# Sums of squares in a gated linear attention: one folded tile and a moved half of a product, in place of two sets of products

## The reference

```python
q, k, v, z = _silu(x @ Wq), _silu(x @ Wk), _silu(x @ Wv), x @ Wz
q, k, v = (causal depthwise convolution over 4 tokens of each)
q = q * cos + rot_half(q) * sin                      # rotary positions, k likewise
q = q / jnp.maximum(jnp.linalg.norm(q, axis=-1, keepdims=True), 1e-12)
k = k / jnp.maximum(jnp.linalg.norm(k, axis=-1, keepdims=True), 1e-12)
for s in range(4):                                   # a token looks at itself and 3 before it
    attn = einsum('bshd,bshd->bsh', q, lag(k, s)) * D ** -0.5
    out = out + (attn * sigmoid(lag(a, s) * b))[..., None] * lag(v, s)
out = out * rsqrt(mean(out * out) + eps) * norm_w * _silu(z)
return out @ Wout
```

## Time and profile before

| | us |
|---|---|
| median of 3 runs | 1094.22 |
| lowest and highest | 1091.1, 1095.05 |
| profiled execution, its own time | 1098.17 |
| its span (first to last instruction) | 1096.4 |
| busy PE, DVE, ACT, POOL in the span | 1013.1, 751.6, 557.3, 285.8 |
| mean granted PE clock | 0.956 |

### The profile page before, as it was taken

How to read it: one execution, slowest core, us unless ns; L and a number is a source line. 1 busy time by engine, 2 the same in 40 slices (tenths; PEclk the granted TensorE clock), 3 DMA queues, 4 the chain that set the end, 5 groups by cost and what they waited for, 6 DMA issues and landing times.

```text
span 1096.4 us, 16891 instructions
## 1 busy us (share of the span) xinstructions
PE 1013.1 (92%) x5736; PEld 804.0 (73%) x5736; DVE 751.6 (69%) x1305; ACT 557.3 (51%) x1105; POOL 285.8 (26%) x246
## 2 busy tenths in 40 slices
PE   6989999999999999999979999999997996679985
PEld 4778988998898854354469989889885454368875
DVE  4778999899899768972377877877874154524333
ACT  2558877877887787711155555655542023022321
POOL 1034234424423401030112122121100005536660
PEclk9989999999999999989989999999998998789996
DMA  7087867877877940430011011110002002178955
GB/s 223 3 218 152 190 154 154 175 163 158 168 162 171 248 106 0 155 86 0 1 58 58 29 57 29 57 57 29 29 0 73 0 1 87 70 222 272 278 159 183
DMA packets 81565, 121.59 MB, mean 111 GB/s; under 512 B 25123, under 2 KB 58734, under 8 KB 80880
## 3 DMA queue, kind: packets, MB, share of 16 engines
q1 hardware_dynamic: 69488, 86.91, 26.5%
q0 software_dynamic: 12032, 34.11, 15.7%
HBM read 70.31 MB, written 38.08 MB: 99 GB/s over the span
## 4 chain that ended last, share of the span: by engine, by line
PE 78%; DVE 10%; DMA 4%; ACT 3%; issue 3%; POOL 2%; SPq 0%; ACTq 0%; POOLq 0%; DVEq 0%
PE psum L647 9%; PE psum L649 9%; PE psum L648 9%; PE psum L872 5%; PE psum L1055 5%; PE psum L701 5%; PE psum L1014 5%; PE psum L819 4%; PE psum L897 3%; PE psum L779 3%; PE psum L760 3%; PE psum L1065 2%; PE psum L828 2%; PE psum L690 2%; DVE arena L1513 2%
## 5 line engine op out<-in xcount | busy, mean ns | idle before, releaser
L1513 DVE SCALAR_TENSOR_TENSOR arena<-arena,par_in 128x1024 f32<-128x1024 f32 x144 | 183.5, 1283 | 33.1 <-ACT arena L1138 23.5
L647 PE MATMUL psum<-G_r,arena_r 128*128 128x512 f32 x320 | 132.8, 415 | 7.2 <-DVE G_r L1606 4.1
L648 PE MATMUL psum<-G_r,arena_r 128*128 128x512 f32 x320 | 127.9, 400 | 0.0
L649 PE MATMUL psum<-G_r,arena_r 128*128 128x512 f32 x320 | 127.7, 399 | 0.0
L1962 POOL DMA_DIRECT2D arena<-arena x64 | 53.8, 983 | 209.3 <-DVE arena L1525 209.2
L1286 ACT ACTIVATE arena<-psum,small 128x256 f32<-128x256 f32 x128 | 59.3, 472 | 87.4 <-DVE small L1671 87.4
L1128 ACT ACTIVATE arena<-psum 128x1024 f32<-128x1024 f32 x48 | 49.2, 1026 | 62.5 <-PE psum L649 61.9
L647 PE MATMUL psum<-arena_r 128*128 128x256 f32 x256 | 78.0, 305 | 2.2 <-DVE arena_r L1696 1.5
L647 PEld LDWEIGHTS psum<-G_r,arena_r 128*128 128x128 f32 x320 | 61.4, 192 | 21.3 <-DVE G_r L1606 4.9
L1978 POOL TENSOR_TENSOR arena_r<-arena,arena_r 128x512 fp32r<-128x512 f32 x16 | 20.7, 1293 | 214.7 <-ACT arena_r L1255 214.7
L2011 POOL DMA_INDIRECT out_rows<-arena x64 | 62.6, 978 | 47.3 <-DVE arena L1856 24.9
(11 more groups left out here) (243 smaller groups left out, 2378.5 us busy)
## 6 DMA issues: line engine op xcount, KB each, us to landing
arena<-arena POOLq DMA_DIRECT2D x64, 256.0 KB, 5.7
arena<-in_w_moe SPq DMA_DIRECT2D x33, 384.0 KB, 3.8
slot_rows<-nowhere SPq DMA_DIRECT2D x16, 576.0 KB, 4.3
arena<-slot_rows SPq DMA_DIRECT2D x32, 288.0 KB, 3.8
arena<-bands SPq DMA_DIRECT2D x16, 528.0 KB, 4.3
sq_rows<-arena POOLq DMA_DIRECT2D x16, 512.0 KB, 7.5
arena<-in_w_qkvz SPq DMA_DIRECT2D x16, 384.0 KB, 4.0
arena<-in_qkv_codes SPq DMA_DIRECT2D x16, 384.0 KB, 3.2
```

Source lines behind the costliest of these rows:

```text
L647: nc.tensor.matmul(dst, w_l, x_h, start=start, stop=False, skip_group_check=True)
L648: nc.tensor.matmul(dst, w_h, x_l, start=False, stop=False, skip_group_check=True)
L649: return nc.tensor.matmul(dst, w_h, x_h, start=False, stop=stop, skip_group_check=True)
L1513: nc.vector.scalar_tensor_tensor(by_batch(dst), by_batch(u[s])[:, :, j:j + S], par_in[:, bass.ds(M_CW + (w * H + h) * TAPS + j, 1)], by_ba ...
```

## The change

Instead of two sets of eight products with ones (k's and q's) PE does one set of eight per head. Three DMAs on POOL's queue make that possible. The first adds the upper 64 partitions of q's squares into the lower 64 (`sqq`). The second adds the lower 64 of k's squares into the upper 64 (`sqk`). The third, once both have landed (`a0_fold`), copies the upper half of `sqk` into the upper half of `sqq` and raises `a0_sq_qk`. The tile `sqq` then holds q's folded squares on partitions 0 to 63 and k's on 64 to 127, and a product with `by_pair` (column 0 ones on the lower half, the other columns ones on the upper half) gives q's sum in column 2i and k's in column 2i+1. `by_pair` lies where a mask of the constants lay and is set by four memsets of DVE in turn 0.

The order changes with it:

- PE: the first half of v's product now comes ahead of k's, the sums (for head h-1, both tensors) behind k's, waiting for `a0_sq_qk`, and the second half of v behind g's transposes.
- DVE: the clamp (`sums_at_least`) moves from ahead of the low half of the weights to behind it, directly ahead of k's convolution; in turn 16 it stays where it was. It writes the columns sorted by tensor again.
- POOL: the two folds come ahead of q's rotation, the copy between q's and k's rotation.
- ACT: the eight copies of v raise a second semaphore after the fourth, and q's next product waits for it half by half. `squared("k")` is written ahead of `lut_act(1)`, but no turn holds both, so no instruction moves.
- SP: the fills (16 of each size) leave the turns of the first attention; they are issued in the second attention's loop, behind `load1(h)`.

```diff
@@ SP, in turn and later @@
-                sp.dma_start(slot_rows...[h], nowhere...).then_inc(sg("moe_fill"), 16)
-                sp.dma_start(out_rows...[h], nil...).then_inc(sg("moe_fill"), 16)
...
+            fill(0)
             with sp.Fori(1, H) as h:
                 sp.wait_ge(sg("a1_wmul"), h)
                 load1(h)
+                fill(h)
@@ PE, project_q @@
-                if since(h, 2):
-                    pe.wait_ge(sg("a0_v_tok"), h - 1)
                 for n in range(2):
+                    if since(h, 2):
+                        pe.wait_ge(sg(("a0_v_tok_lo", "a0_v_tok")[n]), h - 1)
@@ PE, turn @@
-                if 2 in st:
-                    pe.wait_ge(sg("a0_sq_k"), h)
-                    squared_sums(1, "k").then_inc(sg("a0_ssq"), 1)
+                if 1 in st:
+                    pe.wait_ge(sg("a0_silu_q"), h + 1)
+                    project0(slot(0), 2, 0)
...
+                if 2 in st:
+                    if is_last(h, 1):
+                        pe.wait_ge(sg("a_sb"), 7)
+                    pe.wait_ge(sg("a0_sq_qk"), 16 * h)
+                    if since(h, 2):
+                        pe.wait_ge(sg("a0_ssq_s"), h - 1)
+                    for i in range(NT):
+                        m = nc.tensor.matmul(bank(7)[:, 2 * i:2 * i + P], sqq[:, i * P:i * P + P], by_pair,
+                                             start=True, stop=True, skip_group_check=True)
+                    m.then_inc(sg("a0_ssq"), 1)
...
-                    pe.wait_ge(sg("a0_silu_q"), h + 1)
-                    for n in range(2):
-                        i = project0(slot(0), 2, n)
-                    i.then_inc(sg("a0_v"), 1)
+                    project0(slot(0), 2, 1).then_inc(sg("a0_v"), 1)
...
-                if 1 in st:
-                    pe.wait_ge(sg("a0_sq_q"), h + 1)
-                    if since(h, 1):
-                        pe.wait_ge(sg("a0_ssq_s"), h)
-                    squared_sums(0, "q")
@@ DVE, turn @@
-                if 2 in st:
-                    dve.wait_ge(sg("a0_ssq"), h)
-                    ...
+                if is_last(h):
+                    sums_at_least()
...
+                if 2 in st and not is_last(h):
+                    sums_at_least()
+                if 1 in st:
                     conv(1, "k", ck)
@@ POOL, turn @@
                 if 1 in st:
+                    low, high = slice(0, P // 2), slice(P // 2, P)
+                    pool.wait_ge(sg("a0_sq_q"), h + 1)
+                    nc.gpsimd.dma_start(sqq[low, :], sqq[high, :], accum_op=ALU.add).then_inc(sg("a0_fold"), 16)
+                    pool.wait_ge(sg("a0_sq_k"), h + 1)
+                    nc.gpsimd.dma_start(sqk[high, :], sqk[low, :], accum_op=ALU.add).then_inc(sg("a0_fold"), 16)
                     for s in "qk":
+                        if s == "k":
+                            pool.wait_ge(sg("a0_fold"), 32 * (h + 1))
+                            nc.gpsimd.dma_start(sqq[high, :], sqk[high, :]).then_inc(sg("a0_sq_qk"), 16)
```

More of the change, by code:

```diff
@@ L133, in build @@
         ident, ones, inv_d = cst[:, C_ID:C_ID + P], cst[:, C_ONE:C_ONE + P], cst[:, C_INV:C_INV + P]
-        strict = cst[:, C_STRICT:C_STRICT + P]
+        strict, by_pair = cst[:, C_STRICT:C_STRICT + P], cst[:, C_MASK:C_MASK + P]
         half_scale, seam = 0.5 * SCALE, cst[:, C_SEAM:C_SEAM + PAD]
@@ L1559, in turn @@
                     gates_scaled()
+                    for q_rows in range(2):
+                        r = slice(0, P // 2) if q_rows else slice(P // 2, P)
+                        nc.vector.memset(by_pair[r, 0:1], float(q_rows))
+                        i = nc.vector.memset(by_pair[r, 1:P], float(1 - q_rows))
+                    i.then_inc(sg("a_sb"), 1)
                 if 2 in st:
```

37 lines of the change are left out of this document (19 added, 18 removed).

## The result

The changed kernel is **slower**: 1150.2 to 1154.0 us against 1091.1 to 1095.1 us for the kernel before on the same chip, ratio 1.0546, 95% interval 1.0520 to 1.0572. A fourth execution of the changed kernel, at a mean clock of 0.64, took 1467.4 us and is left out. The forecast was 1120 with a range from 1098 to 1140: the direction was right, but the kernel lost some 58 us where 26 were forecast. The profiled execution took 1151.33 us, so its difference from that of the kernel before is 53.2 us, and of the spans (first to last instruction) 52.8.

A forecast was written before the change was run, and what follows sets the result against it. The prediction took PE's own work to bound the kernel, with the ring through the copy bounding it after the change. 8 + 7 + 4 + 8 = +27 us on 1094.2 gave 1121, stated as 1120, range 1098 to 1140.

The forecast's parts named there:

- ring, 14 turns at full clock: First attention's loop, band A to band A through the copy: 21.9 us a turn against 21.3, +8 us.
- PE's clock in them: PE in the loop's turns: half clock after idling ahead of the sums, up to 1.7 us each time, +7 us.
- start: Turns 0 and 1: v's half ahead of k, late rotation and copy, sums at half clock; +4 us, bounds 2 and 5.5.
- end: Turn 16: PE waits for the copy with seven output products queued behind it; +8 us, bounds 4 and 10.
- I take 4 turns: PE's clock in the loop: falls in 4 turns, between never (0) and every turn (24 us); +7 us.
- the clock falls in nearly every turn: Rival, loop turns: half clock costs +24 in place of +7, 1138 us; chance 0.14, shared with a dear copy.
- Its second figure: Rival of clock lost in nearly every turn, plus a copy of 2.2 us: +14 more, 1150 us; within the 0.14.
- the steps: Rotation landing 9.9, copy 1.2, start 0.1, sums 2.05, clamp 0.1, convolution 8.1, wait for v's tap 0.4: 21.9 us.
- upper bound for k's fold: Loop's DMA queues: k's fold moves beside the band's load and may delay q's rotation, +0.5 us a turn at most.
- The copy, behind it in the same queue: Loop, POOL's queue: the copy follows q's second rotation and lands 1.2 us behind it, between 0.6 and 2.2.
- Nothing is won: SP's queue: moving the 13 MB of fills out of the first attention's turns gains 0 us.
- v's half: Turn 0: v's first half ahead of k makes everything behind k's product about 1 us later; counted in the start.

The follow-up runs named there:

- experiment 1: Changed kernel with ten unread 128x128 products on PE ahead of its wait for the copy, heads 2 to 15: 1131.6 us, ratio 1.0350.
- experiments 2 and 4: Changed kernel without the copy: 1090.9 us, ratio 0.9973; changed kernel with q and k squared early and the copy ahead of q's rotations: 1096.9 us, ratio 1.0030.
- Experiment 5: Changed kernel with only ACT's squares early: 1139.2 us, ratio 1.0430; with only the copy issued ahead of q's rotations: 1132.8 us, ratio 1.0360.
- experiment 7: Fills back in changed kernel's turns: 1169.8 us; in early-squares, early-copy, last-head-by-ones kernel: 1107.8. Kernel before with fills moved: 1099.7; with v's first half ahead of k: 1105.8.
- squares-early kernel: Changed kernel with ACT squaring q and k early, the copy still issued behind q's rotations: 1139.2 us, ratio 1.0430.
- experiment 6: Changed kernel with early squares, early copy and last head's sums by ones: 1087.6 us, ratio 0.9952; also with v's first half behind k in turn 0: 1088.5, 0.9908.

## Why the prediction was wrong

By the places of its own sum, in the profiled executions:

| | forecast | measured |
|---|---|---|
| ring, 14 turns at full clock | +8 | +18 (experiment 1) |
| PE's clock in them | +7 | +21 (experiment 1) |
| start | +4 | +3.4 |
| end | +8 | +13.1, less 2.8 behind it |
| all | +27 | +52.8 |

**What held.** The bound moved from PE to the ring band A, sine, rotation, copy, sums, clamp, convolution, band A, and experiments 2 and 4 show it from both sides: without the copy, or with it early, a turn is 20.3 to 20.5 us. In the turn shown the rotation landed at 10.2 us (9.9 in the forecast), the copy at 11.4 (11.1). PE idled 2.22 us there and 2.5 on the mean of the 14 turns (2.4). The price of a half clock per turn was taken as up to 1.7; it is 1.5. The place of the end's loss was right.

**The step that failed: "I take 4 turns".** PE's clock fell in 13 of the 14 turns, and this cost 21 us and not 7 (experiment 1). The prediction had the idle time right, and its nearest rows spoke for the loss: after 2.09 us the clock fell, after 1.60 it did not the earlier trace rows. 2.4 lies beyond the one on which it fell, the turns of the loop are much alike, and still I took a number of turns between "never" and "always" that no row supports. These are 14 us of the missing 26; with them the profiled execution would have been put at 1139 and still have been 12 short, which the ring and the end account for. The rival with that mechanism, "the clock falls in nearly every turn" at 1138, was in a group that held a chance of 0.14, and deserved more. Its second figure, 1150 with a copy of 2.2 us, meets the measured time, and its terms are near: clock +24 for 21, ring +22 for 18. That the sum fits so closely is partly luck, since the end was 5 us longer than in it.

**The ring was short by 0.7 us a turn**, 10 us. At full clock (experiment 1) the sums start 11.7 us behind A on the mean, where the steps gave 11.2, and the rest of the ring takes 10.9 and not 10.7. Experiment 5 shows whose the 0.5 is: with early squares the sums start at 11.2, and the three turns at full clock took 22.14, 22.06 and 21.63 us, where the same turns of experiment 1, with the change's late square of k, took 22.84, 22.64 and 22.20. The prediction named 0.5 as the upper bound for k's fold "with q's rotation behind both", and did not carry it in its sum. In the turn shown the fold was in flight for 7.0 us beside the load of the band and q's rotation, the rotation landed 0.3 later, and the copy was not even issued before 8.3 us (7.2 to 9.7 in turns 2 to 14). "The copy, behind it in the same queue" was wrong as a mechanism: its issue on POOL waited for the fold of k.

**The end** was short by 5. The copy was taken at 1.2 us there too; in turn 16 it was issued 8.7 us after the band A, again after k's fold of 7.0 us, and took 8.5 us beside the loads of w_out and the index tables. PE's sums start 17.2 us behind A, where the steps gave 14.8, and last 3.57 us to the next start, at half clock, where 1.8 was taken. What follows A times v is 2.8 us shorter.

**"Nothing is won" by the fills** was wrong for this kernel (some 18 us, experiment 7) though right for the kernel before: their cost was judged by the old path, on which no DMA stood. Had they stayed, the forecast would have missed by some 44 us and not 26. **The start** came out near its forecast by two errors: with the fills in place band A of turn 1 is 5.4 us late (78.5 and 73.2), and their move gave 2.0 back; that the two nearly cancel is luck. **v's half** was priced for the start alone; in the kernel before it costs 7.5 us over the turns (experiment 7). What it costs in the changed kernel, no run shows by itself.

The Trainium skill's section that the prediction weighed ("DMA: Bandwidth & Descriptors", Anatomy of one DMA) would have the queued copy at 0.6 us behind its neighbour. Where nothing held its issue, in the squares-early kernel, it landed 1.1 us behind the second rotation (10.1 and 11.2 us behind A), which is between the page's 0.6 and the adding DMA's 2.2.

## What to carry to other kernels

Taking work from the engine that bounds pays only if what replaces it comes off the path: before moving a sum to a DMA, add up the ring from one turn to the next, every issue with what its own engine waits for, and ask how early the data could start; here a turn with the same three DMAs takes 24.1 or 20.5 us, depending on where two squares and one issue stand. If the bounding engine is TensorE and would then idle in every turn by about as much as in a row after which its clock fell, price the half clock in nearly every turn, and test it by putting work that nobody reads into the gap: the length of the idle time alone did not decide here. A transfer that was free beside the old path must be priced again once a DMA stands on the new one.

## What the runs showed of the hardware

- Ten products that nobody reads, put into the idle time, kept the clock at 1.00 and made the kernel some 20 us faster (experiment 1).
- The length of one idle time does not decide by itself. In the squares-early kernel idle times of 1.89 to 2.22 us were followed by half clock in 11 turns and those of 1.70, 1.71 and 1.88 us were not; in the changed kernel, where 13 of 2.03 to 3.56 us were, one of 2.44 us was not:

```profile
187.60 2.05 PE L726 MATMUL psum<-cst,arena 128*128 128x128 f32 x16 [2.44 <-DMA arena<-arena]
187.60:191.00 3.40, 3.40 (x27) 3.31 (x28) 2.00 (x4) 0.49 (x2) 1.04 (x1) 1.00 1.03 120
```

  What tells the two apart, no run here shows.
- DMAs of the same 256 KB took very different times to land. In the changed kernel's loop the fold of q took 3.5 to 4.9 us; the fold of k, from turn 2 on beside the load of the band and q's rotation, took 5.5 to 8.5; the copy took 3.1 us in the turn shown and 8.5 in turn 16, beside the loads of w_out and the index tables. The size alone does not tell the time to landing; what else is in flight has to be read with it.
- The ratio to the kernel before may depend on the chip by some tenths of a per cent: the kernel before took 1091.3 us on one and 1099.1 on another, while experiment 6's two versions, on the same two chips, differ by 0.9 us. They also differ by an edit, so this is not shown.
